# A four-layer gated cross-attention network: attention handed over head by head, opening loads and context loads regrouped

## The reference

```python
x = x + jnp.tanh(g_xattn[0]) * _L0_xattn_ref(_layernorm(x), ctx_1024, mask_BxS2_bk0, ...)    # one head
x = x + jnp.tanh(g_ffn[0]) * _L0_ffn_ref(_layernorm(x), ...)                                 # mixture of 8 experts
x = x + jnp.tanh(g_xattn[1]) * _L1_xattn_ref(_layernorm(x), ctx_1024, ctx_1024, mask_BxSxS2_fk0)
x = x + jnp.tanh(g_ffn[1]) * _L1_ffn_ref(_layernorm(x), ...)                                 # searched network
x = x + jnp.tanh(g_xattn[2]) * _L2_xattn_ref(_layernorm(x), ctx_1024, ctx_1024, mask_BxS2_bf1, ...)   # 16 heads
x = x + jnp.tanh(g_ffn[2]) * _L2_ffn_ref(_layernorm(x), ...)                                 # ternary weights
x = x + jnp.tanh(g_xattn[3]) * _L3_xattn_ref(_layernorm(x), ctx_1024, ctx_1024, mask_BxSxS2_ik1, ...)
x = x + jnp.tanh(g_ffn[3]) * _L3_ffn_ref(_layernorm(x), ...)                                 # routed experts

def _L2_xattn_ref(q, k, v, key_padding_mask, Wq, bq, Wk, bk, Wv, bv, Wo, bo):
    qh = (q @ Wq.T + bq).reshape(B_, Lq, 16, 16).transpose(0, 2, 1, 3)      # kh and vh in the same way
    scores = jnp.einsum('bhqd,bhkd->bhqk', qh, kh) / jnp.sqrt(16.0)
    attn = jax.nn.softmax(jnp.where(km, scores, -jnp.inf), axis=-1)
    out = jnp.einsum('bhqk,bhkd->bhqd', attn, vh)
    return out.transpose(0, 2, 1, 3).reshape(B_, Lq, D) @ Wo.T + bo
```

## Time and profile before

| | us |
|---|---|
| median of three runs | 3888.84 (3881.78 to 3891.1) |
| the profiled execution | 3894.26 |
| its span, first to last instruction | 3892.6 |
| PE busy / DVE busy / ACT busy | 3127.2 / 2113.8 / 1362.3 |
| mean granted TensorE clock | 0.901 of full speed |

### The profile page before, as it was taken

One profiled execution on the slowest core, in us unless ns is written; L12 is line 12 of the kernel. 1 busy time (PEld: TensorE's weight loads), 2 busy tenths in 40 slices (PEclk: granted clock), 3 DMA queues, 4 the chain that ended last, 5 costly groups with the idle time before them and its releaser, 6 DMA issues. The chain is left out here.

```text
span 3892.6 us, 62711 instructions
## 1 busy us (share of the span) xinstructions
PE 3127.2 (80%) x24068; PEld 2487.5 (64%) x24068; DVE 2113.8 (54%) x4618; ACT 1362.3 (35%) x2561; POOL 766.9 (20%) x1028
## 2 busy tenths in 40 slices
PE   5854559990667999999999997788888885484979
PEld 4753335650446899999999996466666663253767
DVE  2314421113542778778778775455555556674555
ACT  1321101110221455555555554455555551121000
POOL 2314410005540001301201203111111112273000
PEclk9985679995787999999999998899999996697879
DMA  6561111112553000000000000100000000163000
GB/s 170 159 192 64 38 44 54 43 44 74 153 162 118 1 2 2 2 2 2 2 2 2 2 1 1 47 17 17 17 17 17 17 13 5 31 182 120 12 10 17
DMA packets 123939, 182.43 MB, mean 47 GB/s; under 512 B 14269, under 2 KB 98180, under 8 KB 123438
## 3 DMA queue, kind: packets, MB, share of 16 engines
q1 hardware_dynamic: 110464, 162.96, 13.9%
q0 software_dynamic: 6912, 14.51, 1.3%
q10 hardware_dynamic: 6286, 1.15, 0.2%
HBM read 150.98 MB, written 29.62 MB: 46 GB/s over the span
## 5 line engine op out<-in xcount | busy, mean ns | idle before, releaser
L2059 ACT ACTIVATE probs<-probs,neg_top 112x375 f32<-112x375 f32 x512 | 277.8, 598 | 141.8 <-DVE neg_top L2006 141.8
L2006 DVE CUSTOM_DVE_ANT_0 probs<-ps,add 112x375 f32<-112x375 f32 x512 | 249.9, 545 | 121.5 <-PE ps L2130 121.4
L2157 PE MATMUL ps<-ident,probs 112*125 112x112 f32 x1536 | 216.2, 277 | 57.7 <-DVE probs_t L2013 44.2
L2157 PEld LDWEIGHTS ps<-ident,probs 112*125 112x125 f32 x1536 | 199.1, 190 | 92.9 <-ACT probs L2059 68.6
L2608 PE MATMUL ps<-we,xn_t 128*112 128x256 f32 x1024 | 231.0, 390 | 17.0 <-DVE x_sb L2577 17.0
L1557 DVE TENSOR_REDUCE top<-ps 112x16 f32<-112x1792 f32 x96 | 194.4, 2025 | 60.0 <-PE ps L1773 58.4
L2608 PEld LDWEIGHTS ps<-we,xn_t 128*112 128x112 f32 x1024 | 186.8, 183 | 60.5 <-DVE x_sb L2577 17.8
L1147 DVE TENSOR_TENSOR hidden<-gated,ps 128x512 f32<-128x512 f32 x64 | 44.0, 688 | 309.8 <-PE ps L1190 309.8
L1573 DVE TENSOR_TENSOR probs<-probs,inv_sum 112x1792 f32<-112x1792 f32 x96 | 194.4, 2025 | 3.3
L1561 DVE TENSOR_TENSOR probs<-ps,top 112x1792 f32<-112x1792 f32 x96 | 194.3, 2024 | 3.3
L1569 DVE TENSOR_REDUCE row_sum<-probs 112x16 f32<-112x1792 f32 x96 | 193.9, 2020 | 3.2 <-ACT probs L1659 3.2
(11 more groups left out here) (383 smaller groups left out, 6426.6 us busy)
## 6 DMA issues: line engine op xcount, KB each, us to landing
ctx_t<-in_ctx_T_dram SPq DMA_DIRECT2D x128, 375.0 KB, 12.2
ctx_sb<-in_ctx_dram SPq DMA_DIRECT2D x104, 375.0 KB
queue<-zeros SPq DMA_DIRECT2D x32, 256.0 KB, 3.8
rows<-queue SPq DMA_DIRECT2D x16, 512.0 KB, 4.7
outputs<-out SPq DMA_DIRECT2D x16, 512.0 KB, 3.1
mask_in<-in_mask_BxSxS_fk_dram SPq DMA_DIRECT2D x32, 164.1 KB, 14.1
mask_in<-in_mask_BxSxS_ik_dram SPq DMA_DIRECT2D x32, 164.1 KB, 13.4
we<-in_L_ffn_We_dram SPq DMA_DIRECT2D x18, 256.0 KB, 6.0
```

What stands on the lines that cost most here:

```text
L2006: dve.tensor_tensor_reduce(out=probs[:, u, h, :], in0=k.ps[0:S, SCORE + h, 0:L], in1=add[:, j % 2, :], scale=1.0, scalar=BIG, op0=ALU.add, ...
L2059: act.activation(probs[:, u, h, :], probs[:, u, h, :], ACT.Exp, bias=neg_top[:, u, h:h + 1], scale=-1.0).then_inc(s["probs_done"], 1)
L2157: mm = pe.transpose(k.ps[0:KR, PT + h, r * S:(r + 1) * S], probs[:, n % 3, 2 * half + h, r * KR:(r + 1) * KR], k.ident[0:S, 0:S])
```

## The change

Four things change.

1. **Many-headed attention, handover by head.** `transpose_probs` now signals after each head. Heads 0 and 2 go through bank PT and are copied by DVE (`copy_even`, a copy of 125x336 for each), heads 1 and 3 through PT + 1 and are copied by ACT (`copy_odd`). PE waits ahead of each head for the copy that frees its bank. 
2. **Its pieces moved.** PE's middle piece now stands ahead of `attend(n - 3)`. On DVE `mask_scores(n)` stands ahead of `residual`, and `statistics` moves to u = 3. On ACT the exponentials of heads 2 and 3 of unit n - 1 are taken at the start of unit n, and `copy_raw` stands later.
3. **First attention.** The block of `begin` loads only x and `ctx_t` for j = 0 and 1 and the padding mask on SP, and the first two `ctx_sb` on ACT; the rest of the opening loads is issued in the second block, x and `ctx_t` by SP, six `ctx_sb` by ACT ahead of its first copy. PSUM is dealt out anew: the transposed probabilities have one bank in place of two, `project_out` has two in place of one.
4. **Context loads by ACT.** In first and masked attention the reload of a `ctx_sb` buffer is issued by ACT at the end of an iteration, no longer by SP.

```diff
@@ begin, sync
-                for j in range(NB):
+                for j in range(2):
                     sp.dma_start(k.x_sb[:, 2 * j:2 * j + 2, :], ...).then_inc(k.x_loaded[j], 16)
-                    if j < 4:
-                        sp.dma_start(w.ctx_t[:, j, :, :], ...).then_inc(w.ctx_t_loaded[j], 16)
-                    sp.dma_start(k.ctx_sb[:, j, :, :], ...).then_inc(k.ctx_first[j], 16)
-                    if j == 1:
-                        sp.dma_start(w.pad[:, :], ...).then_inc(k.pad_loaded, 16)
-                sp.dma_start(k.x_sb[:, BODY:B, :], ...).then_inc(k.x_rest_loaded, 16)
+                    sp.dma_start(w.ctx_t[:, j, :, :], ...).then_inc(w.ctx_t_loaded[j], 16)
+                sp.dma_start(w.pad[:, :], ...).then_inc(k.pad_loaded, 16)
@@ first_attention
-        XNT, Q, SCORE, PT, ATT, OUT = 0, 1, 2, 4, 6, 7
+        XNT, Q, SCORE, PT, ATT, OUT = 0, 1, 2, 4, 5, 6
...
+                def load_ctx(j):
+
+                    act.wait_ge(s["att_done"], j - NB + 1)
+                    act.dma_start(k.ctx_sb[:, j % NB, :, :], ...).then_inc(ctx_loaded[j % NB], 16)
...
-                    if j:
-                        pe.wait_ge(s["residual_done"], j)
+                    if j >= 2:
+                        pe.wait_ge(s["residual_done"], j - 1)
                     for c in range(DC):
-                        mm = pe.matmul(k.ps[0:S, OUT, 0:D], ...)
+                        mm = pe.matmul(k.ps[0:S, OUT + j % 2, 0:D], ...)
@@ many_headed_attention, vector
+                    if 0 <= n < N:
+                        mask_scores(n)
                     if u == 0 and 0 <= j - 2 < B:
                         residual(j - 2)
-                    if 0 <= n < N:
-                        mask_scores(n)
                     if 0 <= n - 2 < N:
-                        copy_front(n - 2)
-                    if u == 0 and j + 2 < B:
-                        statistics(j + 2)
+                        copy_even(n - 2, 0)
...
+                    if 0 <= n - 2 < N:
+                        copy_even(n - 2, 2)
+                    if u == 3 and j + 3 < B:
+                        statistics(j + 3)
@@ many_headed_attention, tensor
-                    pe.wait_ge(s["probs_done"], UNIT * n + 2 * half + 2)
-                    if half:
-                        pe.wait_ge(s["front_copied"], n + 1)
-                    elif n:
-                        pe.wait_ge(s["back_copied"], n)
-                    for h in range(2):
+                    for h in range(2 * half, 2 * half + 2):
+                        pe.wait_ge(s["probs_done"], UNIT * n + h + 1)
+                        if 2 * n + half:
+                            pe.wait_ge(s["odd_copied" if h % 2 else "even_copied"], 2 * n + half)
                         for r in range(KC):
-                            mm = pe.transpose(k.ps[0:KR, PT + h, ...], probs[:, n % 3, 2 * half + h, ...], ...)
-                    mm.then_inc(s["back_transposed" if half else "front_transposed"], 1)
+                            mm = pe.transpose(k.ps[0:KR, PT + h % 2, ...], probs[:, n % 3, h, ...], ...)
+                        mm.then_inc(s["head_transposed"], 1)
```

More of the change, by code:

```diff
@@ L128, in _ @@
                 act.dma_start(bo[:, :], row(k.inputs["L0_xattn_bo"]).partition_broadcast(S)).then_inc(columns_loaded, 16)
+                for j in range(2):
+                    act.dma_start(k.ctx_sb[:, j, :, :], k.inputs["ctx_1024"][j].rearrange("(r c) d -> r c d", c=KC)).then_inc(k.ctx_first[j], 16)
                 act.dma_start(k.gates[:, 0:4], row(k.inputs["g_xattn"]).partition_broadcast(P)).then_inc(gates_loaded, 16)
@@ L214, in _ @@
             def _(sp):
[L215 to L224 removed]
+                for j in range(NB):
+                    if j >= 2:
+                        sp.dma_start(k.x_sb[:, 2 * j:2 * j + 2, :], k.inputs["x"][2 * j:2 * j + 2].rearrange("b s d -> s b d")).then_inc(k.x_loaded[j], 16)
+                    if 2 <= j < CT:
+                        sp.dma_start(w.ctx_t[:, j, :, :], k.ctx_t_dram[j].rearrange("(c p) l -> p c l", p=P)).then_inc(w.ctx_t_loaded[j], 16)
+                for j in range(CT, B):
+                    sp.wait_ge(s["scores_done"], j - CT + 1)
+                    sp.dma_start(w.ctx_t[:, j % CT, :, :], k.ctx_t_dram[j].rearrange("(c p) l -> p c l", p=P)).then_inc(w.ctx_t_loaded[j % CT], 16)
+                    if j == CT:
+                        sp.dma_start(k.x_sb[:, BODY:B, :], k.inputs["x"][BODY:B].rearrange("b s d -> s b d")).then_inc(k.x_rest_loaded, 16)
+                    else:
+                        sp.dma_start(fill[j - CT - 1], k.zeros[:, :]).then_inc(k.queue_zeroed, 16)
+                for n in range(B - CT - 1, B):
+                    sp.dma_start(fill[n], k.zeros[:, :]).then_inc(k.queue_zeroed, 16)
                 for j in range(NB):
@@ L312, in residual @@
                     dve.wait_ge(s["out_done"], j + 1)
-                    dve.scalar_tensor_tensor(x, k.ps[0:S, OUT, 0:D], gain[:, j:j + 1], x, ALU.mult, ALU.add).then_inc(s["residual_done"], 1)
+                    dve.scalar_tensor_tensor(x, k.ps[0:S, OUT + j % 2, 0:D], gain[:, j:j + 1], x, ALU.mult, ALU.add).then_inc(s["residual_done"], 1)
                 for j in range(GROUP):
@@ L374, in copy_att @@
                     act.activation(att_t[:, u, :, :], k.ps[:, ATT, 0:DC * S].rearrange("p (c q) -> p c q", c=DC), ACT.Copy).then_inc(s["att_copied"], 1)
+                def load_ctx(j):
+                    act.wait_ge(s["att_done"], j - NB + 1)
+                    act.dma_start(k.ctx_sb[:, j % NB, :, :], k.inputs["ctx_1024"][j % B].rearrange("(r c) d -> r c d", c=KC)).then_inc(ctx_loaded[j % NB], 16)
+                for j in range(2, NB):
+                    act.dma_start(k.ctx_sb[:, j, :, :], k.inputs["ctx_1024"][j].rearrange("(r c) d -> r c d", c=KC)).then_inc(k.ctx_first[j], 16)
                 copy_xn(0)
@@ L541, in _ @@
                         load_ctx_t(j + CT)
-                    if j >= LAG and j - LAG < B:
-                        load_ctx(j - LAG + NB)
                 for j in range(NB):
@@ L2097, in _ @@
                     j, u = divmod(n, UNITS)
-                    if u == 2 and 0 <= j - 1 < B:
-                        copy_raw(j - 1)
+                    if 0 <= n - 1 < N:
+                        exp(n - 1, 1)
                     if 0 <= n < N:
@@ L2105, in _ @@
                         copy_k(j + 1, 1)
+                    if u == 2 and 0 <= j - 1 < B:
+                        copy_raw(j - 1)
                     if u == 3 and 0 <= j - 1 < B:
                         copy_att_t(j - 1)
-                    if 0 <= n < N:
-                        exp(n, 1)
+                    if 0 <= n - 2 < N:
+                        copy_odd(n - 2, 1)
                     if u == 0 and 0 <= j < B:
@@ L2116, in _ @@
                     if 0 <= n - 2 < N:
-                        copy_back(n - 2)
+                        copy_odd(n - 2, 3)
             @block.tensor
@@ L2138, in attend @@
                     pe.wait_ge(s["v2_copied"], j + 1)
-                    pe.wait_ge(s["front_copied"], n + 1)
-                    pe.wait_ge(s["back_copied"], n + 1)
+                    pe.wait_ge(s["even_copied"], 2 * n + 2)
+                    pe.wait_ge(s["odd_copied"], 2 * n + 2)
                     if u == 0 and j:
@@ L2231, in _ @@
                         scores(n)
-                    if 0 <= n - 3 < N:
-                        attend(n - 3)
                     if u == 0 and 0 <= j - 2 < B:
@@ L2241, in _ @@
                         transpose_att(j - 1)
+                    if 0 <= n - 3 < N:
+                        attend(n - 3)
                     if 0 <= n - 2 < N:
```

60 lines of the change are left out of this document (26 added, 34 removed).

## The result

The changed kernel takes **3749.1 us** (median, 3746.6 to 3750.1) against 3885.3 for the kernel before on the same chip: a ratio of 0.9648, 95% interval 0.9632 to 0.9664, or 136 us less.

What follows compares the result with a forecast made beforehand. PE was taken to bound many-headed and first attention, five of sixteen DMA engines masked attention. Terms 53 + 22 + 8 + 0 = 83 us less, from the median 3888.8 to 3806 us; range 3774 to 3856.

Steps and rivals of the forecast that it cites:

- Many-headed attention: Main term: reordering and handover by head remove PE's waits, 1.65 us a batch times 32, 53 us less.
- no visible gap when nothing is late: Many-headed attention: argument against group starts, that PE passes from scores to attend, both with waits, without visible gap.
- The u = 2 wait: Many-headed attention: PE's 0.36 us wait at u = 2, booked on an exponential, was to go.
- The later exponentials: Many-headed attention: heads 2 and 3 taken one unit later, to remove 0.36 us at u = 2.
- hidden with about 1 us to spare: Many-headed attention: ACT's two 450 ns copies a unit cost nothing; ACT reaches its last copy with about 1 us spare.
- Group starts: Rival, many-headed attention: each head's own wait costs PE 0.07 us, 18 us given back, 3824 us; chance 0.15.
- First attention's loop: Term: two banks for project_out remove its wait for residual, 22 us less, 12 if five DMA engines run behind.
- The opening: Term, start of first attention: second block at 18 to 21 us, x[3] lands at about 45; 8 us less.
- the opening pays in full: Rival, opening: SP's ring keeps its share, x[3] there at 31 to 34 us; 20 instead of 8; chance 0.11.
- Masked attention: Term, both masked stages: issuing ctx_sb from ACT gains 0 us, between 4 less and 12 more.
- The reasoning on the five engines: Masked attention: a 125-partition ctx_sb moves on five of sixteen DMA engines, 3.0 us each, setting the pace.
- ACT in the ring: Rival, masked and first attention: ctx_sb issues block ACT and add to its work, 224 us, 4030 us; chance 0.07.

## Why the prediction was wrong

The direction and the places were right. By the stages that it touches the change is worth 139 us (136 by the medians of the whole kernel), where I had 83: many-headed attention has 39 of the 56 us between them, masked attention 11, first attention's loop 7. The miss is above all one term.

- **Many-headed attention, 53 forecast, 91.9 measured.** The step that failed is the price: I took the sum of PE's shown waits as what a batch can gain, and called 67 us, all of them, a bound. By the distances between PE's starts, a batch fell by 2.61 us. Shown waits are 1.81 of it (2.07 to 0.26), where I had 1.65; the other 0.80 is in pieces that start earlier with no wait shown before. In the prediction's own numbers it was in sight: I used 0.98 us for the scores as their length. They take 0.83, and the rest was `attend` waiting for ACT's copy of two heads, partly under the scores' modelled end:

```profile
2708.72 0.90 PE L2130 MATMUL ps<-k_t,q_t 32*112 32x375 f32 x8
2708.83 0.73 ACT L2065 ACTIVATE probs_t<-ps 125x672 f32<-125x672 f32 x1 [0.59 <-PE ps L2157]
2709.70 0.78 PE L2145 MATMUL ps<-probs_t,v 125*32 125x112 f32 x24
```

  The copy ends at 2709.56 and `attend` starts 0.14 later, in three units of four, with no wait shown; what I had read as "no visible gap when nothing is late" was a wait. 0.80 x 32 = 26 us, 0.16 x 32 = 5, and some 8 us lie outside the steady batches: two batches of the trace of before took 25.65 us, the rest is at the stage's two ends.
- **The u = 2 wait** goes, all but some 0.1 us, but by the handover and not by the later exponentials. The later exponentials are worth 17.7 us for another reason, ACT's time for the odd head, where I had 0.36 x 32 = 12. I had called ACT's two shorter copies hidden with about 1 us to spare; they are so only where they stand now.
- **Group starts** (rival, 18 us back): wrong. No group of transposes in a steady batch shows a wait after the change, and most cost less in the end (0.75 us from start to start, against 0.80 to 0.82 for those that had waited), not more. One still waits unseen: at u = 2 the second group starts at 2668.44, 0.15 us after the end of DVE's copy, and itself takes 0.81 us to the next start.
- **First attention's loop, 22 forecast, 28.8 alone.** The same step: 0.82 us shown for an iteration, 1.04 gained. The five DMA engines held nothing back.
- **The opening, 8 forecast, 8.0 measured** (stage), by luck. The block ended 5 us later than I said, for gates behind `ctx_sb`, which I passed over; x[3] was there all the same at 39.35 us and not at about 45, so that the way in which I shared the engines between the two rings was off by some 6 us; and of the 11.9 us gained at `copy_qbk(0)` the stage keeps 8.0. ACT's six issues took 11.85 us, within what I allowed. The rival that the opening pays in full (20 us) didn't come either.
- **Masked attention, 0 forecast, 5.8 and 4.8 less**, 10.6 together and beyond my bound of 4. The reasoning on the five engines was right, but the second ring brought some throughput, 195 in place of 183 GB/s in the windows of layer 1. The Trainium skill, DMA: Bandwidth & Descriptors, section Rules for kernel authors, gives it nothing; these runs give it a little. The stretch up to PE's last piece became 6.8 and 6.9 us shorter, the end with only `ctx_sb` left 1.0 and 2.0 longer.
- **ACT in the ring** (rival, 224 us more): its first half came, as the prediction had it ("ACT's issues grow to 2 us and more"), but not its price. In the first part of each masked stage an issue of `ctx_sb` on ScalarE took 0.26 to 0.42 us, later mostly 1 to 3:

```profile
1032.10 0.42 ACTq L718 DMA_DIRECT2D ctx_sb<-in_ctx_dram  x1
...
1090.10 2.87 ACTq L718 DMA_DIRECT2D ctx_sb<-in_ctx_dram  x1
```

  The stages were shorter even so, so the issue time and the work of an iteration didn't add up. The likely reason, which no run takes by itself, is that ACT stands only where the transfers set the pace anyway.

What stays open: why the masked stages gained 5 us from the second ring, and how the DMA engines share their time between two rings.

## What to carry to other kernels

Price a wait of TensorE by the distance between the starts of its pieces, with the same piece elsewhere as the measure: here a shown wait was short by 0.07 to 0.22 us, and one below 0.07 to 0.16, according to the piece in front, isn't shown. Look for the waits that aren't shown where a copy ends within 0.2 us of PE's next start. Load tiles whose partition count has no large divisor up to 16 in two parts: 125 as 112 and 13 was worth 61 us on masked attention, where the change itself had brought 11.

## What I had not expected of the hardware

- From the last transpose of a group to PE's next group, across a copy of 0.86 us, there are 1.18 us: 0.32 us of the two handovers together.
- With sixteen engines at a share of 0.95 the masked stage moved 239 GB/s, while the expert weights moved 322 at 1.02: both times the engines are full by the share, and the rates differ by a third. That it depends on what they carry is my reading.
